# Moving a 4-byte buffer behind the activation buffer and the row buffers, which then start at multiples of 128 bytes

## The reference

```python
# layer 0: gated two-branch MLP, then a gated feed-forward
norm = where(m, layernorm(x) * (1 + scale) + shift, 0)
h1 = gelu(norm @ ssm_w1 + ssm_b1); h2 = gelu(norm @ bwd_w1 + bwd_b1)
x = x + gate_msa * where(m, h1 @ ssm_w2 + ssm_b2 + h2 @ bwd_w2 + bwd_b2, 0)
h = gelu_tanh((layernorm(x) * (1 + scale_mlp) + shift_mlp) @ ff_w1 + ff_b1)
x = x + gate_mlp * (h @ ff_w2 + ff_b2)
# layer 1: attention with 16 heads of 32, then a feed-forward of 2048
xn = modulate(layernorm(x) * ln1_w + ln1_b)
q, k, v = xn @ wq + bq, xn @ wk + bk, xn @ wv + bv
x = x + softmax(q k^T / sqrt(32)) v @ wo + bo
xn = modulate(layernorm(x) * ln2_w + ln2_b)
x = x + gelu(xn @ w1 + b1) @ w2 + b2
```

## Time and profile before

| | us |
|---|---|
| median of three runs | 1948.76 |
| lowest and highest run | 1947.34 and 1951.3 |
| profiled execution, span from first to last instruction | 1949.1 |
| TensorE busy | 1898.6 |
| VectorE busy | 1230.6 |
| ScalarE busy | 716.5 |
| GpSimd busy | 483.9 |

### The profile page before, as it was taken

The page is one execution under the profiler, slowest core; times in us unless marked ns, Lnnn a source line. Parts: engine busy times, 40 slices in busy tenths (PEclk is TensorE's granted clock), DMA queues, the critical chain, the costliest instruction groups (busy, mean ns, idle before and its releaser), DMA issues.

```text
span 1949.1 us, 33162 instructions
## 1 busy us (share of the span) xinstructions
PE 1898.6 (97%) x11210; PEld 1569.1 (81%) x11210; DVE 1230.6 (63%) x2058; ACT 716.5 (37%) x2106; POOL 483.9 (25%) x577
## 2 busy tenths in 40 slices
PE   5999999999999999999999998899999999999999
PEld 4778888887888778888988887678888888888887
DVE  5677777767767775888888888446262534436222
ACT  3222233332232223777777777232121212112111
POOL 4333333322222222334443443101010101002000
PEclk8999999999999999999999999999999999999999
DMA  8654444444455443678777778512020110202000
GB/s 293 197 171 164 154 153 151 154 145 141 153 158 169 165 140 108 215 250 268 244 246 257 259 246 258 186 63 87 1 87 31 56 54 32 70 16 86 0 22 22
DMA packets 225200, 276.40 MB, mean 142 GB/s; under 512 B 15308, under 2 KB 144936, under 8 KB 225128
## 3 DMA queue, kind: packets, MB, share of 16 engines
q1 hardware_dynamic: 210624, 232.11, 36.0%
q0 software_dynamic: 12160, 39.14, 6.7%
q10 hardware_dynamic: 2344, 4.25, 0.6%
HBM read 175.29 MB, written 100.14 MB: 141 GB/s over the span
## 4 chain that ended last, share of the span: by engine, by line
PE 84%; DMA 6%; DVE 5%; issue 3%; ACT 1%; POOL 1%; ACTq 0%; SPq 0%; DVEq 0%; POOLq 0%
PE wide L675 31%; PE banks L652 31%; PE banks L1452 18%; PE wide L1485 2%; DMA turned_squares<-rows 2%; PE spare L1508 2%; DMA rows<-turned_squares 1%; DVE rows L919 1%; DMA rows<-gate_bias_rows 1%; ACT rows L805 1%; DMA x_tiles<-turned_probs 0%; DVE h L946 0%; DMA x_tiles<-x 0%; DVE rows L922 0%; DVE h L944 0%
## 5 line engine op out<-in xcount | busy, mean ns | idle before, releaser
L675 PE MATMUL wide<-weights,h 128*128 128x512 f32 x3072 | 755.2, 396 | 10.8 <-DVE h L946 10.8
L652 PE MATMUL banks<-xn,weights 128*128 128x512 f32 x3048 | 733.7, 391 | 6.9 <-DVE xn L934 6.1
L675 PEld LDWEIGHTS wide<-weights,h 128*128 128x128 f32 x3072 | 575.4, 188 | 153.2 <-DVE h L946 14.0
L652 PEld LDWEIGHTS banks<-xn,weights 128*128 128x128 f32 x3048 | 573.0, 188 | 132.1 <-DVE xn L934 6.5
L816 ACT ACTIVATE rows<-banks,vecs 128x512 f32<-128x512 f32 x256 | 176.4, 689 | 926.3 <-PE banks L652 897.9
L944 DVE CAST h<-rows 128x512 fp32r<-128x512 f32 x256 | 120.7, 471 | 418.5 <-ACT rows L816 394.6
L805 ACT ACTIVATE rows<-rows,mod_tables 128x128 f32<-128x128 f32 x360 | 148.4, 483 | 140.7 <-DMA rows<-turned_squares 140.2
L1452 PE MATMUL banks<-xn,weights 128*128 128x256 f32 (+1 forms) x1524 | 196.2, 290 | 1.1 <-DVE xn L1764 0.7
L1452 PEld LDWEIGHTS banks<-xn,weights 128*128 128x128 f32 x1524 | 189.2, 193 | 5.9 <-DVE xn L1764 1.5
L946 DVE TENSOR_TENSOR h<-rows,h 128x512 fp32r<-128x512 f32 x256 | 186.5, 729 | 8.8
L1452 PE MATMUL banks<-weights,xn 128*128 128x512 f32 x780 | 188.3, 397 | 3.8 <-DVE xn L1811 2.9
(11 more groups left out here) (132 smaller groups left out, 1492.6 us busy)
## 6 DMA issues: line engine op xcount, KB each, us to landing
turned_squares<-rows SPq DMA_DIRECT2D x124, 256.0 KB, 2.9
rows<-turned_squares SPq DMA_DIRECT2D x124, 256.0 KB, 2.9
turned_probs<-probs_room SPq DMA_DIRECT2D x62, 512.0 KB, 3.2
x_tiles<-x SPq DMA_DIRECT2D x98, 256.0 KB, 3.2
x<-x_tiles SPq DMA_DIRECT2D x96, 256.0 KB, 3.5
rows<-gate_bias_rows POOLq DMA_DIRECT2D x64, 256.0 KB, 4.1
probsT_room<-turned_probs SPq DMA_DIRECT2D x64, 256.0 KB, 4.4
x_tiles<-turned_probs SPq DMA_DIRECT2D x64, 256.0 KB, 4.9
```

Source lines behind the costliest of these rows:

```text
L652: last = nc.tensor.matmul(m1_bank(n, c), st.tiles[0](a, k, c), xn[:, parity, b, k, :], start=s == 0, stop=s == len(steps) - 1)
L675: last = nc.tensor.matmul(y_ps[:, tile, :], h[:, c % 2, a, tile * P:(tile + 1) * P], st.tiles[1](b, c), start=c == 0 and s == 0, stop=c == ...
```

## The change

The buffer `unused` is taken from the stack behind `neg_half` and no longer ahead of `probs_room` and `h`. In the built program `h` and `probs_room` then start at 199808, `rows` at 208000, `neg_half` at 228480 and `unused` at 228512. The small statistics buffers behind them stay where they were, as does everything ahead of 199808. The three large buffers that move now start at multiples of 128 bytes, and half way between two multiples of 256, as the weights, `xn` and `x_tiles` did already. The instructions of each engine, their order and their waits are the same as before.

```diff
         sh.mask = ctx.enter_context(nc.sbuf_tensor("mask", [P, B], F32))
-        sh.unused = ctx.enter_context(nc.sbuf_tensor("unused", [P, 1], F32))
         with nc.sbuf_tensor("probs_room", [P, 2, NSQ, HALF, SQ], F32) as probs_room:
             sh.probs = probs_room[:, :, :, :, :]
         sh.h = ctx.enter_context(nc.sbuf_tensor("h", [P, 2, 2, TOK], F32R))
...
         sh.neg_half = ctx.enter_context(nc.sbuf_tensor("neg_half", [P, 4], F32))
+        sh.unused = ctx.enter_context(nc.sbuf_tensor("unused", [P, 1], F32))
         sh.squares_dram = nc.dram_tensor("turned_squares", (TPB, P, D), F32, kind="Internal").ap()
```

## The result

The changed kernel takes 1932.68 us (median of five runs, 1931.21 to 1933.23), the kernel before 1949.31 us (five runs, 1947.34 to 1951.3). The ratio is 0.991, with a 95% interval of 0.9899 to 0.9921. That is 16.6 us less, where I had forecast no measurable change and had given 0.09 to a gain.

A forecast was written before the change was run, and what follows sets the result against it. TensorE's own time plus 50.5 us of idle time was taken to bound the kernel. The terms for TensorE, VectorE, GpSimd and transfers, each 0, left the median at 1948.8 us, range 1944.5 to 1953.5 us.

The forecast's parts named there:

- no measurable change: Whole kernel: the time stays within about 0.2%, 3.9 us, of before, at 1948.8 us; chance 0.87.
- a gain: Whole kernel: faster by more than 0.2%, from any cause; chance 0.09.
- What bounds the kernel: TensorE is busy 1898.6 of 1949.1 us; an edit can change only matmul costs or its 50.5 us of idle time.
- TensorE's term: L675's 3072 matmuls holding `h`: the slow pace belongs to the streamed operand, so 0, with bounds 0 to -18.4 us.
- the comparison with the attention: Values and projections, holding aligned `xn`, take 8.38 us for 36 matmuls, 232.8 ns each, as slow as L675's 233.1.
- The weight loads: On TensorE, L675's loads of `h` take 188 ns in the median, as L652's loads of an aligned weight do.
- VectorE, GpSimd and the transfers: Accesses to moved buffers outside TensorE: 0 each, bounds -1.0 us, -0.9 us, and -0.8 to +0.8 us.
- The Trainium skill's rule: Transfers from `rows`: 2048-byte pieces cost 69 beats before, 68 after, 64 if aligned to 256; well under 1 us gained.
- The first one: Faster by TensorE's reads of `h`: L675 falls to L652's pace, 18.4 us less, 1930.4 us; chance 0.03.
- The second rival: Attention's end: a shorter `probs_room` transfer keeps TensorE's clock up, 7.0 us less, 1941.8 us; chance 0.06 with similar idle-place causes.
- The third: VectorE at TensorE's idle places: `rows` in step with other buffers collide, 6.2 us more, 1955.0 us; slower has chance 0.04.

## Why the prediction was wrong

**What bounds the kernel** was right, and it is what made the cause easy to find: TensorE's own time or its idle time, nothing else. The gain is all in the first.

**TensorE's term is the step that failed**, with the inference that the slow pace of L675 belongs to which operand is streamed and not to the address of `h`. I put it at 0 with a bound of -18.4 us, and it was the bound that came true: L675 gave 17.7 us of busy time, and its pace fell by 232.9 - 226.7 = 6.2 ns, 3072 x 6.2 = 19.0 us if it held everywhere. What misled me was the comparison with the attention: 36 matmuls of L1452 took 8.38 us, and I read 232.8 ns for each. That quotient is a mean over a stretch that isn't uniform. By the starts in the trace of before, the 35 steps in it are one of 334 ns, four of 228 to 236, and thirty of 226 or 227. The 334 ns lies where the line's run begins, and the 36th step, to the first matmul of the next line, is 318. Its true pace was that of L652. One more view would have told: the median of a single duration, which such steps don't touch. In the trace of before it reads

```profile
L1452 PE MATMUL banks<-weights,xn x780: 387/389/767, 769.3 to 1236.9; 128*128 128x512 f32 x195
```

389 ns, where L675's median was 395:

```profile
L675 PE MATMUL wide<-weights,h x3072: 387/395/504, 36.7 to 1945.4; 128*128 128x512 f32 x192
```

So the trace of before did hold the answer: two products of the same form, held and streamed the same way, 6 ns apart in the median, and of what the prediction had compared only the address differed.

**The weight loads** taking 188 ns in both lines was true and proved nothing: the load's own duration didn't change when the pace did. The cost shows in the matmuls: in their median duration (395 against 389 ns) and in the distance from one to the next.

**L652's part** I had not seen at all. It gave 2.4 us although neither of its operands moved. In the kernel before its twelfth matmul, the last one before L675's loads, stood 235.0 ns from the next and its first 230.8, the ten between 226.6 to 226.7 (means over the complete runs of twelve between 1400 and 1700 us). That looks like a collision between the stream of one matmul and the load for the next one, since at the twelfth it is `h` that is loaded. But the other runs don't bear it out: with `h` off by 64 the twelfth stands at 225.8 ns, and the first six at 228.2 to 236.0. And the twelfth of L675, which streams weights while weights in step with them are loaded, stays slow in the kernel before, at 232.6 ns. So which two accesses meet stays open; what is shown is that the step decides.

**VectorE, GpSimd and the transfers** came out at 0 as forecast. The run with `rows` alone off (1931.83 against 1932.68 us) shows it for every access to `rows` at once.

**The Trainium skill's rule** on pieces that don't start at a multiple of 256 bytes (the page "DMA: Bandwidth & Descriptors", section "How a descriptor splits into AXI transactions") would give the run with everything at multiples of 256 five beats less of 69 than the kernel before. Its quiet transfers from `rows` took 2.0 us, the same as at 160 past a multiple, and its time was that of the changed kernel. An estimate by the page's beats, 5/69 of 2.0 us, is 0.1 us, the last digit of these rows. The single packets are finer: those of 2048 bytes, 8192 of them between 1400 and 1880 us, took 84 ns in the median before, after and with all large buffers at multiples of 256, and 85 with all of them 160 past one, where 5/69 of 84 would be 6 ns. No run here shows the rule's cost.

**The rivals.** The first one had the right place and nearly the right time (1930.4 us against 1932.68), with a chance of 0.03. Its sign, a pace of L675 near 227 ns, came true, but it can't tell an offset of `h` by itself from one relative to the weights. Its reason, the offset of `h` by itself, was half right: the offset matters relative to the weights, and the alignment to 128 bytes that the change is about matters not at all. The second rival didn't occur: TensorE still waits 7.3 us for the probabilities at the end of the attention in the longest case, against 6.8. The third, rows in step with other buffers, had the idea of phase and the wrong sign and engine: it expected equal places to collide on VectorE where no cost was found (L969 at 692 ns as before), while on TensorE unequal places are what costs.

**The chances.** I gave 0.87 to no change, on the strength of a single quotient that excluded the one large term. A term of 18.4 us whose exclusion hangs on one row should have kept a larger chance, and the range should have reached it.

## What to carry to other kernels

In a kernel that TensorE bounds, with products of this form, place the buffers of held and of streamed operands at equal addresses modulo 256 bytes, and look what a tiny buffer ahead of them does; here 4 bytes of scratch, rounded up to 32, cost 0.9% of the time, and being aligned bought nothing. Compare the pace of two products by the median of single durations or by the distances of their starts, not by the length of a run divided by its count alone: in the row that misled me the two steps at the seams (334 and 318 ns) hid a difference of 3%. Where a bound of a cost is large and only one row excludes it, read the same fact from a second view before setting it to zero.

## What the runs showed of the hardware that was not expected

- For float32r products with 128 held columns and 512 streamed ones, at the 2.4 GHz level, the distance between matmuls is 226.7 ns with the two operands in step and 232 to 234 ns at steps of 32, 64, 96, 128, 160 and 224 bytes. The steps 16 and 256 behave as 0.
- The absolute address doesn't matter: all buffers 32 bytes past a multiple of 128 gave 1934.89 us, all at multiples of 256 gave 1932.0, all 128 past one gave 1932.68.
- The disturbance outlasts its cause: matmuls in step that follow a run out of step come back to 226.7 ns only from the eighth of twelve on, in the run with `xn` alone off.
- Products with only 256 streamed columns don't follow this. The keys and queries (L1452, weights held, `xn` streamed) were busy for 188.8 to 190.4 us in the runs where they are in step (189.0 in the changed kernel), and for 185.7 and 186.7 us in the two runs with `xn` 32 bytes off. From start to start between 830 and 1190 us that is 123.3 ns in the mean in the changed kernel, and 121.0 with `xn` alone off. They were faster out of step, by 2%; with the weights 32 bytes off, at a step of 160, they took 188.4 us. Why stays open, as does the mechanism behind the period of 256 bytes.
